# Layer-0 sums as one reduce, dense weights' low parts and last sum at other places, two steps of the first unit whole

## The reference, cut to what matters

```
z0   = x0[b,i,d] * x0[b,j,d]            # 39*39 products per (b, d)
cur0 = relu(z0 @ W0)                    # 128: the first 64 are next_h, the others direct0
z1   = x0[b,i,d] * next_h[b,j,d]        # 39*64 products per (b, d)
cur1 = relu(z1 @ W1)                    # 128
z    = sum over d of concat(direct0, cur1)           # 192 per row
h    = relu(concat(z, dense_ctx) @ W_top1 + b1)      # 208 -> 512
y    = relu(h @ W_top2 + b2) @ W_top3                # 512 -> 256 -> 1
```

## Time and profile before

| | us |
|---|---|
| median of 3 runs (lowest, highest) | 1521.45 (1518.25, 1523.64) |
| the profiled execution | 1519.96 |
| its span, first to last instruction | 1518.1 |
| busy PE, DVE, ACT, POOL in the span | 1440.1, 1397.6, 828.8, 934.8 |

### The profile page before, as it was taken

How to read it: one execution, slowest core, us unless ns; L and a number is a source line. 1 busy time by engine, 2 the same in 40 slices (tenths; PEclk the granted TensorE clock), 3 DMA queues, 4 the chain that set the end, 5 groups by cost and what they waited for, 6 DMA issues and landing times.

```text
span 1518.1 us, 15055 instructions
## 1 busy us (share of the span) xinstructions
PE 1440.1 (95%) x4462; PEld 796.9 (52%) x4462; DVE 1397.6 (92%) x1279; ACT 828.8 (55%) x899; POOL 934.8 (62%) x604
## 2 busy tenths in 40 slices
PE   3179999999999999999999999999999999999989
PEld 2145555555555555555555555555555555555556
DVE  2179999999999999999999999999999999999983
ACT  0155456655655555655655555665665555665645
POOL 7638887868687786868687786868686780000000
PEclk7579999999999999999999999999999999999999
DMA  4067998999989988999998999999899998899600
GB/s 146 6 158 192 226 220 213 207 227 205 217 203 213 212 218 213 206 222 205 215 215 206 207 217 222 206 214 211 212 214 211 214 215 213 208 203 219 177 11 1
DMA packets 137290, 292.96 MB, mean 193 GB/s; under 512 B 37646, under 2 KB 62878, under 8 KB 137080
## 3 DMA queue, kind: packets, MB, share of 16 engines
q1 hardware_dynamic: 102642, 278.35, 76.9%
q0 software_dynamic: 19200, 4.95, 2.8%
q10 hardware_dynamic: 15366, 8.70, 2.1%
HBM read 283.95 MB, written 7.87 MB: 192 GB/s over the span
## 4 chain that ended last, share of the span: by engine, by line
PE 68%; DVE 18%; issue 7%; another core or an unknown queue 3%; DMA 1%; SPq 1%; ACT 0%; DVEq 0%
PE psB L487 32%; PE psA L487 10%; DVE z L893 7%; PE psB L512 5%; DVE z_lo L902 5%; PE psB L505 5%; DVE z_split L893 5%; PE psB L508 4%; PE psA L495 2%; PE psB L495 1%; PE psA L505 1%; PE psA L508 1%; PE psA L512 1%; DMA x_lay<-x_rows 1%
## 5 line engine op out<-in xcount | busy, mean ns | idle before, releaser
L466 POOL DMA_INDIRECT emb<-in_tbl,ids_all x600 | 934.6, 1558 | 317.7 <-issue 178.7
L487 PE MATMUL psB<-z,w 128*128 128x512 f32 x1536 | 689.3, 595 | 3.2 <-DVE z L893 3.0
L758 ACT ACTIVATE z_hi<-z_split 128x1024 fp32r<-128x1024 f32 (+1 forms) x288 | 304.0, 1059 | 471.4 <-DVE z_split L893 395.5
L487 PEld LDWEIGHTS psB<-z,w 128*128 128x128 f32 x1536 | 292.4, 191 | 360.5 <-issue 343.6
L893 DVE TENSOR_TENSOR z<-h_quad,x_lay 128x1024 f32<-128x1024 f32 x352 | 417.8, 1217 | 5.9 <-PE psB L487 4.3
L902 DVE TENSOR_TENSOR z_lo<-z_split,z_hi 128x1024 fp32r<-128x1024 f32 (+1 forms) x288 | 351.9, 1222 | 4.8 <-ACT z_hi L758 4.1
L893 DVE TENSOR_TENSOR z_split<-h_quad,x_lay 128x1024 f32<-128x1024 f32 x224 | 270.4, 1220 | 0.7 <-DVE z_lo L902 0.7
L712 ACT ACTIVATE h_quad<-psA 32x1024 f32<-32x1024 f32 x248 | 251.9, 1016 | 3.7
L487 PE MATMUL psA<-z,w 126*128 126x512 f32 x512 | 240.7, 592 | 0.0
L505 PE MATMUL psB<-z_hi,w_hi 128*128 128x512 f32 x448 | 158.9, 436 | 1.6 <-issue 1.6
L487 PEld LDWEIGHTS psA<-z,w 126*128 126x128 f32 x512 | 96.8, 189 | 97.5 <-issue 90.4
(11 more groups left out here) (113 smaller groups left out, 868.1 us busy)
## 6 DMA issues: line engine op xcount, KB each, us to landing
x_lay<-x_rows SPq DMA_DIRECT2D x1152, 128.0 KB
x_more<-x_rows SPq DMA_DIRECT2D x62, 504.0 KB
bases<-x_rows SPq DMA_DIRECT2D x62, 468.0 KB
x_lay<-x_rows SPq DMA_DIRECT2D x64, 256.0 KB
x_ring<-x_rows SPq DMA_DIRECT2D x31, 504.0 KB
emb<-in_tbl,ids_all POOLq DMA_INDIRECT x600
x_last<-x_rows SPq DMA_DIRECT2D x64, 128.0 KB
x_rows<-x_side ACTq DMA_DIRECT2D x58, 120.0 KB
```

Source lines behind the costliest of these rows:

```text
L466: nc.gpsimd.indirect_dma_start(emb[t % 2][:, f * D:(f + 1) * D], None, tables[f], bass.IndirectOffsetOnAxis(ids_all[:, t, f:f + 1], 0)).th ...
L487: mm = nc.tensor.matmul(ps[:, cs], w[0:k, :], z[WHOLE_NO[place] % NZ][0:k, cs], start=first, stop=last)
L758: nc.scalar.activation(z_hi[n % NS][0:k, 0:cols], z_split[n % NS][0:k, 0:cols], ACT.Copy).then_inc(z_hi_made, 1)
```

## The change

Four edits. (1) ACT writes `r0` as (row, d), as r1 already is, and the layer-0 sum is one `tensor_reduce` of 2048 columns into 128. (2) Steps 2 and 3 of layer 1 are whole in unit 0 (`EARLY`, `split1`); w1 has two more columns of weights. (3) `dense_low` stands behind step 15 of unit 0 instead of step 1. (4) In the last unit `split_top` stands behind step 17 instead of 15 and makes three parts; the fourth (`split_top2`, weights of the second dense layer) and the last layer-0 sum stand behind the loop, between `feat_low(0)` and the last layer-1 sum. SP's move waits for the first part only; PE waits for three parts ahead of the first dense product, and for the fourth ahead of the second layer.

```diff
-WHOLE1 = tuple(s for s in range(STEPS1) if s not in SPLIT1)
+EARLY = (2, 3)
+WHOLE1 = tuple(s for s in range(STEPS1) if s not in SPLIT1 or s in EARLY)
...
+def split1(u):
+    return tuple(s for s in SPLIT1 if u > 0 or s not in EARLY)
...
-            sp.wait_ge(top_lo_made, 4)
+            sp.wait_ge(top_lo_made, 1)
...
-                elif s in SPLIT1:
+                elif s in split1(u):
...
-            pe.wait_ge(top_lo_made, 4)
+            pe.wait_ge(top_lo_made, 3)
...
                     top1(i + 1)
+                if i == 0:
+                    pe.wait_ge(top_lo_made, 4)
...
-                nc.scalar.activation(half(r0, u)[rows, :], h[H:P, :], ACT.Relu).then_inc(relu0_done, 1)
+                by_d = h.rearrange("p (d b) -> p b d", b=P)[H:P]
+                nc.scalar.activation(r0_by_b[rows, :, u % 2 * DH:(u % 2 + 1) * DH], by_d, ACT.Relu).then_inc(relu0_done, 1)
...
-            def sum_over_d(r, n):
-                width = C
-                for step in range(3):
-                    nc.vector.tensor_tensor(r[:, 0:width], r[:, 0:width], r[:, width:2 * width], ALU.add).then_inc(sum_step, 1)
-                    dve.wait_ge(sum_step, 3 * n + step + 1)
-                    width //= 2
...
             def sum0(q):
                 dve.wait_ge(relu0_done, 4 * q + 4)
-                sum_over_d(r0, q)
-                add_last(r0, feat_d, q * P, sum0_done)
+                nc.vector.tensor_reduce(feat_d[:, q * P:(q + 1) * P], r0_by_b, AX.X, ALU.add).then_inc(sum0_done, 1)
...
-                part(w_top_lo, slice(0, P), slice(2 * M1, 2 * C), w_top[0][:, 2 * M1:])
+
+            def split_top2():
+                cs = slice(2 * M1, 2 * C)
+                nc.vector.tensor_tensor(w_top_lo[:, cs], w_top[0][:, cs], w_top_hi[:, cs].bitcast(FP), ALU.subtract).then_inc(top_lo_made, 1)
...
-                    if s == 15 and u == UNITS - 1:
+                    if s == 17 and u == UNITS - 1:
                         split_top()
...
-                    if s == 1 and u == 0:
+                    if s == 15 and u == 0:
                         dense_low()
...
-                    if s == STEPS1 - 2 and u % 4 == 3:
+                    if s == STEPS1 - 2 and u % 4 == 3 and u < UNITS - 1:
                         sum0(u // 4)
...
             feat_low(0)
+            split_top2()
+            sum0(UNITS // 4 - 1)
             sum1(TILES - 1)
```

More of the change, by code:

```diff
@@ L112, in at1 @@
     return STEPS0 + STEPS * u + s + sum(a < s for a in after(u))
-WHOLE_AT = sorted([at0(u, s) for u in range(UNITS) for s in WHOLE0] + [at1(u, s) for u in range(UNITS) for s in WHOLE1])
-SPLIT_AT = sorted([at0(u, s) for u in range(UNITS) for s in SPLIT0] + [at1(u, s) for u in range(UNITS) for s in SPLIT1])
+def split1(u):
+    return tuple(s for s in SPLIT1 if u > 0 or s not in EARLY)
+SPLIT_AT = sorted([at0(u, s) for u in range(UNITS) for s in SPLIT0] + [at1(u, s) for u in range(UNITS) for s in split1(u)])
+WHOLE_AT = sorted([at0(u, s) for u in range(UNITS) for s in WHOLE0] +
+                  [at1(u, s) for u in range(UNITS) for s in range(STEPS1) if s not in split1(u)])
 WHOLE_NO = {place: n for n, place in enumerate(WHOLE_AT)}
@@ L211, in tower @@
         half_spread = [r1[:, c * C:c * C + BANK].rearrange("p (d r) -> p d r", d=DH) for c in range(2)]
-        r1_by_b = r1[:, :].rearrange("p (b d) -> p b d", d=D)
+        r0_by_b, r1_by_b = [t[:, :].rearrange("p (b d) -> p b d", d=D) for t in (r0, r1)]
         def lay(u, m):
@@ L292, in tower @@
         relu1_done = sem("relu1_done")
-        sum_step = sem("sum_step")
         sum0_done = sem("sum0_done")
@@ L765, in body @@
                         keep_x(u + 2)
-                    if s in SPLIT1:
+                    if s in split1(u):
                         high(at1(u, s))
@@ L949, in low_before @@
                     low(place - 1)
-            def sum_over_d(r, n):
-                width = C
-                for step in range(3):
-                    nc.vector.tensor_tensor(r[:, 0:width], r[:, 0:width], r[:, width:2 * width], ALU.add).then_inc(sum_step, 1)
-                    dve.wait_ge(sum_step, 3 * n + step + 1)
-                    width //= 2
-            def add_last(r, feat, col, done):
-                nc.vector.tensor_tensor(feat[:, col:col + P], r[:, 0:P], r[:, P:2 * P], ALU.add).then_inc(done, 1)
             def sum0(q):
                 dve.wait_ge(relu0_done, 4 * q + 4)
-                sum_over_d(r0, q)
-                add_last(r0, feat_d, q * P, sum0_done)
+                nc.vector.tensor_reduce(feat_d[:, q * P:(q + 1) * P], r0_by_b, AX.X, ALU.add).then_inc(sum0_done, 1)
             def sum1(t):
```

## The result

The changed kernel takes 1511.94 us (median of 5 runs, 1509.67 to 1512.72), the kernel before beside it 1521.68: ratio 0.9934, interval 0.9918 to 0.995. The forecast was 1512.5. By the medians the gain is 9.7 us. The profiled execution took 1511.94 us with a span of 1510.1, so 8.0 us less span than before.

The account below looks back on a forecast made before the run. PE was taken to bound the steady part, with DVE hardly behind. Gains of 2.3 + 2.7 + 3.9 = 8.9 us took the profiled 1519.96 to 1511.1; with the median 1.5 above, 1512.5 was forecast, range 1509 to 1518.

Parts of the forecast that it names:

- The reduce: Layer-0 sums in the steady part: DVE held 2.27 instead of 2.70 us, PE's lateness behind seven sums goes, 2.3 us.
- Rival C: ACT's strided copy of r0 takes twice 1.02 us and makes DVE late in each unit: slower, 1531 us; chance 0.03.
- The tail: Last unit: no PE wait at the last low part, no clock fall, everything from the layer-1 sum 3.9 us earlier.
- Rival B: Last unit gives 2 us only, as the clock falls again in PE's new wait: 1514.5 us; chance 0.08.
- The start-up: Units 0 and 1: whole steps 2 and 3 and the moved dense low part let PE leave 2.7 us ahead.
- step 4: Layer 1 of unit 0 on PE: starts at 117.5 instead of 120.87 us, 3.4 us ahead.
- step 16's wait: Unit 0, behind the moved dense low part: PE waits 0.2 to 0.3 us for this step.
- h_quad: ACT's copies for unit 1, held until both dense low parts are done: start at 142.8 us instead of 144.23.
- the high part: ACT's next high part in unit 1, behind the held copies: at 154.4 us instead of 155.78.
- the product behind the old wait: PE's product behind the start-up wait of 178.88: at 176.7 us, not 179.4.
- DVE regains something: Unit 1: x_lay loads come 3.4 us earlier, DVE's waits for them go, step 5 at 162.3 instead of 165.01 us.
- Rival A: Start-up gives nothing, as ACT's held copies or the loads take it back in unit 1: 1515.3 us; chance 0.14.

Follow-up runs that it names:

- after: First measurement and profile of the changed kernel, all four edits against the kernel before: 1511.94 us, ratio 0.9934.
- after_again: The changed kernel run once more, unchanged, against the kernel before on the same chip: 1512.03 us, ratio 0.9929.
- x_sum: The kernel before with only the layer-0 sum as one reduce and r0 written as (row, d): 1519.9 us, ratio 0.9976.
- x_start: The kernel before with steps 2 and 3 of unit 0 whole and the dense low part behind step 15: 1518.89 us, ratio 0.9977.
- x_early: The kernel before with steps 2 and 3 of unit 0 whole, dense low part left behind step 1: 1520.08 us, ratio 0.9987.
- y_best: The changed kernel with unit 2's half loads behind unit 1's x_lay loads and another order behind the loop, on another chip: 1474.87 us, ratio 0.9937.

## Why the prediction was right, and where it was not

- **The reduce: 2.3 forecast, 1.8, 2.1 and 2.25 measured** (after, after_again, x_sum). Mechanism and size held; the middles without the reduce lie between 1233.62 and 1234.20, so a few tenths either way are the spread of single profiles. Rival C, the dear copy, is dead at 1.021 us. The Trainium skill (VectorE: DVE Perf Modes, Rules for kernel authors) calls tensor_reduce the slowest DVE operation; here one reduce of 2048 columns took 2.274 us on the mean of 8 and held DVE for 2.20, against 2.70 for the four adds.
- **The tail: 3.9 forecast, 3.8 measured**, with each step in place: no wait at the low part, the layer-1 sum 2.3 us behind PE's end (2.2 forecast; PE's end is 1451.82 and five products of 1.72 us, since the record at 1460.08 starts before its turn), and 1.06 us of wait for the forecast 1. Rival B didn't come. But the forecast took the fallen clock as given. Of seven profiles with the old tail five had the fall (69.15 to 69.47 us) and two did not (67.75 and 67.73). So about 1.5 of the 3.8 us is a fall that the old tail takes in some runs, and against a run without it the edits save 2.4. The Trainium skill (TensorE: Matmul & The Clock Gate, HAM oscillation) warns of the fall behind an idle PE; here the same idle time had it and had it not.
- **The start-up: 2.7 forecast, 1.80, 1.88 and 1.67 measured** (after, after_again, x_start). This is the term that was mis-sized. By the clock times of the changed kernel's profile most of its walk held: step 4 at 117.74 (117.5), step 16's wait 0.29 (0.2 to 0.3), h_quad at 143.24 (142.8), the high part at 154.74 (154.4), the product behind the old wait at 177.08 (176.7). But here the first product came 0.57 us earlier than before, at 103.79, and step 4 did not: counted from the first product step 4 is 2.56 us ahead and not 3.4. The granted clock was low later in this profile, from 109 to 112 us, while the forecast had the low clock end at 111.0 (x_start has the late low clock too, and step 4 2.52 us ahead). after_again has the first product and the low clock as before, and step 4 3.37 us ahead (117.58), as forecast. There the step that failed is "DVE regains something ... they come 3.4 us earlier": PE leaves the start-up 1.88 us ahead. The loads behind unit 2's store came 1.7 us earlier in SP's queue than before (150.26 against 151.93; 149.38 in the other profile), and DVE still waits for them in after_again:

```profile
163.20 1.23 DVE L902 TENSOR_TENSOR z<-h_quad,x_lay 128x1024 f32<-128x1024 f32 x1 [0.64 <-DMA x_lay<-x_rows]
```

  The store was 3.3 us earlier (131.59 against 134.88), but 27 issues stand between it and these loads. They took 18.7 us instead of 17.1 (17.6 in the other profile), and from 144 us on the DMA engines are full. A window of the changed kernel:

```profile
150.00:156.00 6.00, 6.00 (x15) 2.65 (x14) 3.75 (x5) 5.90 (x9) 4.96 (x4) 1.00 1.07 228
```

  The forecast looked at the share between 132 and 135 us to say that nothing held the loads; the window that counts comes some ten microseconds later. Rival A named both takers rightly. x_early shows the loads taking all of the lead, the other chip shows ACT's hold taking 2.0, and in the changed kernel the two end close together: one profile waits for the loads and the other, with the smaller lead, does not.
- **The sum**, 8.9 by the forecast, is 7.4 by the stretches and 8.0 by the span. The forecast of the median came within 0.6 us of the result, and that is in part luck: it added 1.5 us for the distance of median and profiled execution, which were equal after the change, and this reserve took up the 1.5 us by which the sum was too high.

## What to carry over

Where a lead is to be carried from one stage to the next, follow the loads of the next stage through the queue and read the DMA share where they fly, not where they are released. An edit can be worth next to nothing until a second one joins it: whole steps alone gave 0.1 us of start-up, with the moved dense part 1.7 (one profile each, and the dense part alone was not measured where it could be compared). A reduction in one instruction can beat a tree of adds whose total column count is lower. A stage that single profiles show up to 1 us apart, as this start-up is, needs more than one profile before the parts of a sum are judged in it.

## What the runs showed of the hardware

- Behind one and the same PE wait of 3.13 to 3.18 us the granted clock fell to 0.50 to 0.57 (the lowest window of 2 us; 0.50 is the lower of its two levels, 1.2 GHz) in five profiles and stayed at 1.00 in two. The tail was 1.4 to 1.7 us longer with the fall.
- On one chip the first product started at 57.3 to 59.1 us, on the others at 102.5 to 105.3. The waits up to 104 us of the kernel before, then those up to 60 us of y_best on that chip (engine, line, what is waited for: us, times, longest):

```profile
DVE z L1052 <- remote: 45.3, 4, 18.5
PE psB L554 <- issue: 25.4, 2, 24.6
```
```profile
PE psB L562 <- DVE x_lay L1042: 7.6, 2, 6.8
```

  In the stretch from 20 to 45 us of the kernel before, PE is busy for 2.16 of 25 us with the DMA share at 0.07; in y_best for 14.30 with 0.31. The profile names no instruction or load that ends these waits, waits of DVE on `remote` of 24.6 to 49.5 us stand in every profile of the other chips, and no run here tells their cause. Nine of the 46 us are lost again in the start-up (88 to 90 us there); the whole program is 37 us shorter, nearly four times what this change brings.
